# Hyperbolic attention: a constant product beside the points' products, inverses taken once per row and head, and half of batch 1's logarithms moved among batch 0's weights

## The reference

```python
q_hyp = _expmap0(qn)
k_hyp = _expmap0(kn)
inner = -jnp.einsum('bhti,bhsi->bhts', q_hyp[..., :1], k_hyp[..., :1]) + jnp.einsum('bhtd,bhsd->bhts', q_hyp[..., 1:], k_hyp[..., 1:])
mdot = jnp.maximum(-inner, 1.0 + 1e-06)
dist = jnp.arccosh(mdot)
scores_hyper = -(dist * dist) / curv_k
scores = (1.0 - alpha) * scores_euclid + alpha * scores_hyper
scores = jnp.where(causal[None, None], scores, -jnp.inf)
attn = jax.nn.softmax(scores, axis=-1) * spike_mask
y = jnp.einsum('bhts,bhsd->bhtd', attn, v)
```

## Time and profile before

| | us |
|---|---|
| runs of the kernel before | 2789.78, 2783.0, 2782.54 (median 2783.0) |
| the profiled execution: time, span | 2787.06, 2785.2 |
| TensorE busy in the span | 2356.0 (85%) |
| VectorE busy | 1455.3 (52%) |
| ScalarE busy | 1055.5 (38%) |
| POOL busy | 382.4 (14%) |
| the changed stage | 1560.4 to about 1664.3 of the span |

### The profile page before, as it was taken

The page is one execution under the profiler, slowest core; times in us unless marked ns, Lnnn a source line. Parts: engine busy times, 40 slices in busy tenths (PEclk is TensorE's granted clock), DMA queues, the critical chain, the costliest instruction groups (busy, mean ns, idle before and its releaser), DMA issues. The chain is left out here.

```text
span 2785.2 us, 38678 instructions
## 1 busy us (share of the span) xinstructions
PE 2356.0 (85%) x15024; PEld 1366.0 (49%) x15024; DVE 1455.3 (52%) x2285; ACT 1055.5 (38%) x1896; POOL 382.4 (14%) x659
## 2 busy tenths in 40 slices
PE   3999999868999598999996675976879799698778
PEld 1344444435699363444543442441227657364447
DVE  4777777323221366888881873335666433223333
ACT  2566666412111234777773561224222233021310
POOL 2453000000000300000001520003430000000100
PEclk8899999987999797999998677987688899898779
DMA  6976544020353898555430001001004430200200
GB/s 189 246 185 160 103 92 62 1 95 1 150 220 129 249 288 221 96 117 104 88 46 33 12 1 58 28 1 62 0 0 154 166 149 1 93 3 0 99 0 8
DMA packets 108213, 258.59 MB, mean 93 GB/s; under 512 B 11808, under 2 KB 83072, under 8 KB 94080
## 3 DMA queue, kind: packets, MB, share of 16 engines
q1 hardware_dynamic: 101696, 203.71, 27.7%
q0 software_dynamic: 2736, 39.37, 4.2%
q10 hardware_dynamic: 3600, 13.04, 1.2%
HBM read 211.26 MB, written 44.83 MB: 92 GB/s over the span
## 5 line engine op out<-in xcount | busy, mean ns | idle before, releaser
L666 DVE TENSOR_REDUCE sta_parts<-sta_psA 128x1 f32<-128x1024 f32 x544 | 625.7, 1187 | 186.9 <-PE sta_psA L583 185.2
L724 ACT ACTIVATE sta_probs<-sta_psS 128x512 f32<-128x512 f32 x1056 | 575.8, 596 | 274.2 <-PE sta_psS L594 272.1
L594 PE MATMUL sta_psS<-L_xattn_qS,L_xattn_kst 99*128 99x256 bf16 x2112 | 355.8, 278 | 11.5 <-ACT sta_probs L724 6.6
L583 PE MATMUL sta_psA<-L_xattn_kst,L_xattn_qS 99*128 99x512 bf16 x1088 | 293.2, 387 | 45.9 <-PEq L59 31.0
L594 PEld LDWEIGHTS sta_psS<-L_xattn_qS,L_xattn_kst 99*128 99x128 bf16 x2112 | 161.2, 98 | 259.3 <-ACT sta_probs L724 183.6
L603 PE MATMUL sta_psO<-sta_probs,L_xattna_V 128*32 128x256 f32 x2560 | 189.5, 385 | 0.0
L583 PEld LDWEIGHTS sta_psA<-L_xattn_kst,L_xattn_qS 99*128 99x128 bf16 x1088 | 104.2, 99 | 130.5 <-DVE sta_parts L666 43.8
L202 ACT ACT_TABLE_LOAD x14 | 18.0, 1283 | 331.6 <-PEq L59 331.6
L2385 PE MATMUL l2t_psY<-l2t_hc,top_consts_weights 128*128 128x512 f32 x128 | 96.4, 863 | 26.7 <-DVE l2t_hc L2436 26.6
L603 PE MATMUL sta_psO<-sta_probs,L_xattn_V 128*32 128x256 f32 x1536 | 114.5, 389 | 0.0
L1008 ACT ACTIVATE sht_probs<-sht_psS 128x768 f32<-128x768 f32 (+1 forms) x64 | 55.3, 864 | 148.6 <-PE sht_psS L852 99.8
(11 more groups left out here) (625 smaller groups left out, 3967.2 us busy)
## 6 DMA issues: line engine op xcount, KB each, us to landing
L_xattn_kst<-L_xattn_keys SPq DMA_DIRECT2D x186, 136.0 KB, 4.9
L_xattn_kst<-L_xattn_keys SPq DMA_DIRECT2D x186, 128.0 KB, 4.5
L_xattn_values<-prj_rows SPq DMA_DIRECT2D x64, 256.0 KB, 3.8
L_xattn_keys<-prj_parts SPq DMA_DIRECT2D x32, 384.0 KB, 4.0
L_xattna_V<-in_ctxV SPq DMA_DIRECT2D x5, 2048.0 KB, 11.8
L_xattna_V<-L_xattn_values SPq DMA_DIRECT2D x5, 2048.0 KB, 11.0
l2f_W<-in_M SPq DMA_DIRECT2D x10, 1024.0 KB, 7.6
L_xattn_keys<-sta_bparts SPq DMA_DIRECT2D x24, 384.0 KB, 7.3
```

Source lines behind the costliest of these rows:

```text
L583: last = nc.tensor.matmul(psA[:, u % 2, col:col + rhs.shape[1]], lhsT, rhs, start=True, stop=True)
L594: last = nc.tensor.matmul(psS[:, at % 2, j * T:(j + 1) * T], lhsT, rhs, start=True, stop=True)
L666: nc.vector.tensor_reduce(into(parts[:, u // n % 2]), view(psA[:, u % 2, :]), AX.X, ALU.max).then_inc(max_taken, 1)
L724: nc.scalar.activation(probs[:, u % NP, i * 512:(i + 1) * 512], psS[:, at % 2, :], ACT.Exp, scale=scale).then_inc(probs_ready, 1)
```

## The change

It does four things. First, the spikes are no longer spread at the start; the tile spikesT, the copy and the 512-column spreading are gone. Second, behind each pair's points' products TensorE multiplies the constant bf16 mask (128 x 512) by the identity, twice, into psY, where nobody reads it. Third, normalisation goes another way: TensorE makes the row sums of a quad as a 128 x 8 tile with queries on partitions (`sums`), VectorE takes the reciprocal of that and multiplies it by the spikes in two small operations (`invert`), ScalarE copies it to 128 x 256 with each number repeated 32 times (`widen`), TensorE turns that with two transposes (`spread`), and VectorE multiplies by yP (`scale`). psY now has one buffer, whose other half takes the sums, and psN has one. Fourth, ScalarE takes Ln of pairs 8 to 11 ahead of Exp of pair 4; only pairs 12 to 15 are left for after batch 0's weights.

```diff
@@ -1873,12 +1874,12 @@
         D = p.sb("D", [P, B * H, W])
         R = p.sb("R", [P, B * H, W])
         top = p.sb("top", [P, PAIRS, TB, 2])
-        spikesT = p.sb("spikesT", [P, NTOK])
         yP = p.sb("yP", [P, 2, T])
-        inverse = p.sb("inverse", [P, 2, T])
+        inverse = p.sb("inverse", [P, 2, TB, 4])
+        wide = p.sb("wide", [P, 2, T])
         banks = p.ps("banks", [P, 2 * SLOTS, 512])
-        psY = p.ps("psY", [P, 2, T])
-        psN = p.ps("psN", [P, 2, T])
+        psY = p.ps("psY", [P, 512])
+        psN = p.ps("psN", [P, T])
 
         def pair(kind, k):
             n = place[kind, k] % SLOTS
...
@@ -1935,29 +1936,35 @@
                     pe.wait_ge(turn_copied, 2 * g + 2)
                     if g:
                         pe.wait_ge(y_copied, g)
+                        pe.wait_ge(inverse_in, g)
                     b = g // (QUADS // B)
                     for kt in range(TB):
                         for j in range(4):
                             h = 4 * (g % (QUADS // B)) + j
-                            last = nc.tensor.matmul(psY[32 * j:32 * j + 32, g % 2, kt * P:T], v[:, b * TB + kt, 32 * h:32 * h + 32],
+                            last = nc.tensor.matmul(psY[32 * j:32 * j + 32, kt * P:T], v[:, b * TB + kt, 32 * h:32 * h + 32],
                                                     R[:, 4 * g + j, kt * T:kt * T + T - kt * P], start=kt == 0, stop=kt == TB - 1)
                     last.then_inc(y_ready, 1)
 
-                def spread_sums(g):
+                def sums(g):
+
                     pe.wait_ge(y_copied, g + 1)
+                    for t in range(TB):
+                        last = nc.tensor.matmul(psY[:, T + 4 * t:T + 4 * t + 4], yP[:, g % 2, t * P:(t + 1) * P], K["col32"], start=True, stop=True)
+                    last.then_inc(sums_ready, 1)
+
+                def spread(g):
+                    pe.wait_ge(widened, g + 1)
                     if g:
-                        pe.wait_ge(inverted, g)
-                    else:
-                        pe.wait_ge(spikes_copied, 1)
-                    nc.tensor.matmul(psN[:, g % 2, :], K["sel32"], yP[:, g % 2, :], start=True, stop=True).then_inc(spread_ready, 1)
-
-                for t in range(NT):
-                    last = nc.tensor.matmul(psN[:].rearrange("p a n -> p (a n)")[:, t * P:(t + 1) * P], spikes[:, t:t + 1].to_broadcast([P, P]), K["ident"],
-                                            start=True, stop=True)
-                last.then_inc(spikes_spread, 1)
+                        pe.wait_ge(scaled, g)
+                    for t in range(TB):
+                        last = nc.tensor.matmul(psN[:, t * P:(t + 1) * P], wide[:, g % 2, t * P:(t + 1) * P], K["ident"], start=True, stop=True)
+                    last.then_inc(spread_ready, 1)
+
                 for k in range(PAIRS):
                     slot_free("hyper", k)
                     products(pair("hyper", k), turned["qH"], turned["kH"], k, True).then_inc(hyper_ready, 1)
+                    for _ in range(2):
+                        nc.tensor.matmul(psY[:], K["ident16"], K["mask16_q"], start=True, stop=True)
                 for b in range(B):
                     first, end = b * HALF, (b + 1) * HALF
                     scores(first)
@@ -1968,10 +1975,14 @@
                         turn(k)
                         if k % 2 == 0 and k > first:
                             values(k // 2 - 1)
+                        if k % 2 == 0 and k > first + 2:
+                            spread(k // 2 - 2)
                         if k % 2 and k > first + 1:
-                            spread_sums((k - 3) // 2)
+                            sums((k - 3) // 2)
                     values(end // 2 - 1)
-                    spread_sums(end // 2 - 1)
+                    spread(end // 2 - 2)
+                    sums(end // 2 - 1)
+                    spread(end // 2 - 1)
 
             @block.vector
             def _(dve):
@@ -1985,14 +1996,19 @@
                     dve.wait_ge(reach_ready, k + 1)
                     V.scalar_tensor_tensor(out=both(R, k), in0=pair("hyper", k), scalar=1.0, in1=both(D, k), op0=ALU.add, op1=ALU.mult).then_inc(root_in, 1)
 
-                def normal(g):
+                def invert(g):
+                    b = g // (QUADS // B)
+                    dve.wait_ge(sums_ready, g + 1)
+                    V.reciprocal(inverse[:, g % 2], psY[:, T:T + 4 * TB].rearrange("p (t h) -> p t h", t=TB)).then_inc(inverse_in, 1)
+                    dve.wait_ge(inverse_in, g + 1)
+                    for t in range(TB):
+                        last = V.tensor_scalar(inverse[:, g % 2, t], inverse[:, g % 2, t], spikes[:, b * TB + t:b * TB + t + 1], None, ALU.mult)
+                    last.then_inc(inverted, 1)
+
+                def scale(g):
                     b, c = g // (QUADS // B), g % (QUADS // B)
                     dve.wait_ge(spread_ready, g + 1)
-                    V.reciprocal(inverse[:, g % 2, :], psN[:, g % 2, :]).then_inc(inverted, 1)
-                    dve.wait_ge(inverted, g + 1)
-                    V.tensor_tensor(inverse[:, g % 2, :], inverse[:, g % 2, :], spikesT[:, b * T:(b + 1) * T], ALU.mult).then_inc(inverse_ready, 1)
-                    dve.wait_ge(inverse_ready, g + 1)
-                    V.tensor_tensor(attT[:, c, b * T:(b + 1) * T], yP[:, g % 2, :], inverse[:, g % 2, :], ALU.mult).then_inc(scaled, 1)
+                    V.tensor_tensor(attT[:, c, b * T:(b + 1) * T], psN[:], yP[:, g % 2, :], ALU.mult).then_inc(scaled, 1)
 
                 reach(0)
                 for k in range(PAIRS):
@@ -2014,10 +2030,15 @@
                         for t in range(TB):
                             last = V.tensor_reduce(top[:, k, t, :], both(D, k)[:, :, cols[t]], AX.X, ALU.max, negate=True)
                         last.then_inc(top_ready, 1)
-                        if k % 2 and k >= first + 5:
-                            normal((k - 5) // 2)
-                    normal(end // 2 - 2)
-                    normal(end // 2 - 1)
+                        if k % 2 == 0 and k >= first + 4:
+                            invert(k // 2 - 2)
+                        if k % 2 == 0 and k >= first + 6:
+                            scale(k // 2 - 3)
+                    invert(end // 2 - 2)
+                    scale(end // 2 - 3)
+                    scale(end // 2 - 2)
+                    invert(end // 2 - 1)
+                    scale(end // 2 - 1)
                 dve.wait_ge(scaled, QUADS)
 
             @block.gpsimd
@@ -2037,8 +2058,8 @@
                         act.wait_ge(root_in, k + 1)
                         nc.scalar.activation(line(R, k), line(R, k), ACT.Sqrt).then_inc(root_ready, 1)
 
-                def logarithms(b):
-                    for k in range(b * HALF, (b + 1) * HALF):
+                def logarithms(pairs):
+                    for k in pairs:
                         act.wait_ge(sum_ready, k + 1)
                         nc.scalar.activation(line(D, k), line(D, k), ACT.Ln, bias=K["ones"][:, 0:1]).then_inc(log_ready, 1)
 
@@ -2050,11 +2071,18 @@
                     act.wait_ge(y_ready, g + 1)
                     if g >= 2:
                         act.wait_ge(scaled, g - 1)
-                    nc.scalar.copy(yP[:, g % 2, :], psY[:, g % 2, :]).then_inc(y_copied, 1)
+                    nc.scalar.copy(yP[:, g % 2, :], psY[:, 0:T]).then_inc(y_copied, 1)
+
+                def widen(g):
+                    act.wait_ge(inverted, g + 1)
+                    nc.scalar.copy(wide[:, g % 2, :].rearrange("p (x n) -> p x n", n=32),
+                                   inverse[:, g % 2].rearrange("p t h -> p (t h)").unsqueeze(2).to_broadcast([P, 4 * TB, 32])).then_inc(widened, 1)
 
                 def weights(b):
                     first, end = b * HALF, (b + 1) * HALF
                     for k in range(first, end):
+                        if b + 1 < B and k == first + HALF // 2:
+                            logarithms(range(end, end + HALF // 2))
                         act.wait_ge(top_ready, k + 1)
                         for j in range(2):
                             for t in range(TB):
@@ -2065,16 +2093,18 @@
                             copy_turned(k - 1)
                             if k % 2 and k > first + 1:
                                 copy_y((k - 3) // 2)
+                            if k % 2 and k >= first + 5:
+                                widen((k - 5) // 2)
                     copy_turned(end - 1)
+                    widen(end // 2 - 2)
                     copy_y(end // 2 - 1)
-
-                act.wait_ge(spikes_spread, 1)
-                nc.scalar.copy(spikesT[:], psN[:].rearrange("p a n -> p (a n)")).then_inc(spikes_copied, 1)
+                    widen(end // 2 - 1)
+
                 roots(0)
-                logarithms(0)
+                logarithms(range(HALF))
                 roots(1)
                 weights(0)
-                logarithms(1)
```

(13 more changed lines are left out.)

## The result

| | before | after |
|---|---|---|
| median of the runs, us | 2782.77 (2781.08 to 2789.78) | 2808.96 (2806.4 to 2827.57) |
| ratio after/before, 95% interval | | 1.0110 (1.0077 to 1.0142) |
| profiled execution, span, us | 2785.2 | 2804.2 |
| stage, from the first product to attT's last write, us | 103.8 | 126.7 |

A forecast was written before the change was run, and what follows sets the result against it. VectorE was taken to bound the points' products, and chains between engines the weights. Batch 0's +8.4 us (holding the opening's -0.9) and batch 1's +6.3 make +14.7: median 2783.0 to 2797.7 us (2792.9 to 2800.4); range with rivals 2787 to 2809.

The forecast's parts named there:

- part 3: Normalisation in both batches: VectorE saves 1.65 us per quad, but inverses wait for sums and spreadings for widening.
- Part 1: Opening and constant products: TensorE at 2.4 GHz, added matmuls hidden in its waits, Exp of pair 0 0.9 us earlier.
- the cold opening: Rival: TensorE at 1.2 GHz from the first pairs bounds the opening; total +26 us, 2809; chance 0.12.
- Part 2: Ln of pairs 8 to 11 ahead of Exp 4: +5.3 us there, 3.4 us back in the later block.
- A drain beside each load: Skill page's rule, weighed: about 1.38 us on top of each ScalarE table load; sum +17.4 us instead of +14.7.
- the chain of batch 0: Batch 0's weights from Exp 4 through quad 3's widening: 22.5 us, mostly at 1.2 GHz, against 16.0 before.
- the all-1.2 GHz value of 23.5: Batch 0's weights from Exp 4 to widen 3 if TensorE ran at 1.2 GHz throughout: 23.5 us; 19.8 at 2.4.
- the string: Step-by-step times of waits between engines, counted from Exp 4 in batch 0 and from Exp 8 in batch 1.
- The bound all at 1.2 GHz: Batch 1 from Exp 8 to the end, with 1.2 GHz from spread 4 on: 39.7 us; 38.0 was taken.
- Waits hidden: Rival: ScalarE packs Ln into idle time and TensorE's new waits lie beside other work; +1.9 us, 2785; chance 0.15.
- faster: Rival: waits hidden and VectorE's 1.65 us less per quad counts where it is gapless; -4.1 us, 2779; chance 0.08.
- the rival with more waits: Rival: more waits between engines than the prediction strung together; +18 to +22 us; chance 0.05.

The follow-up runs named there:

- reordered: The changed kernel with all its operations, normalisation steps put one or more pairs later, four buffers instead of two for yP, inverse and wide; stage 104.89 us, ratio 0.9993.
- transposed: The changed kernel with the two products of each spreading made as transposes instead of fp32 matmuls; stage 120.05 us, ratio 1.0061.
- clock_held: The changed kernel with further constant products wherever TensorE waits, ahead of the spreadings and of turns 0, 4 and 8; stage 110.40 us, ratio 1.0019.
- fill_before: The kernel before with constant products behind each pair's products and 20 and 26 more ahead of the batches' first turns; stage 94.04 us, ratio 0.9985.
- change_again: The changed kernel, unaltered, measured a second time against the kernel before; stage 126.70 us, median 2811.44 us, ratio 1.0076.
- norm_alone: The kernel before with only the new normalisation in the change's order and no spikes' spreading; no constant products, no moved Ln; stage 119.95 us, ratio 1.0049.
- fill_reordered: The reordered kernel with 20 and 26 constant products ahead of the first turns of batches 0 and 1; run twice, stages 99.04 and 99.02 us, ratio 0.9979 both times.
- fill_reordered_noln: The reordered kernel with constant products ahead of the first turns and Ln of pairs 8 to 11 not moved; stage 91.64 us, ratio 0.9952.

## Why the prediction was wrong in size, point by point

**Direction and mechanism: right.** Slower, by the two waits strung together in part 3, with VectorE's reciprocals waiting for TensorE and the spreadings for ScalarE. Undoing the order (reordered) takes 21.8 of the 22.8 us back, the clock's part included.

**Part 1: right.** Exp 0 was to come 0.9 us earlier, and came 0.87 (33.83 against 34.70). The clock held at 1.00 in the first part; the cold opening did not come. Which of the reasons that I gave for it held the clock, no run separates. That TensorE would be idle over 4 us ahead of turn 0 and start the weights at 1.2 GHz was right too: 4.35 us, and 0.55 in the row of 1592 to 1596.

**Part 2: right.** Exp 4 at 1612.25 (forecast 1612.5). The later block, from the last widening to Exp 8, took 6.02 (5.95). A drain beside each load was set aside on 1.31 us before, and the kernel after has the same:

```profile
1638.05 3.41 ACT L2064 ACTIVATE hyp_D<-hyp_D,top_consts_weights 128x768 f32<-128x768 f32 x4
...
1641.48 1.28 ACT L2090 ACT_TABLE_LOAD   x1
...
1642.77 1.49 ACT L2090 ACTIVATE hyp_D<-hyp_D,hyp_top 128x128 f32<-128x128 f32 x4
```

From the last Ln's end, 1641.46, to Exp 8 lie 1.31 us. By "ScalarE: Activation LUTs" in the Trainium skill, section "What ACT_TABLE_LOAD costs", it would be 2.66; no run here shows a drain.

**Part 3: the step that failed is the size of the chain.** Exp 8 was forecast at 1641.0 and came at 1642.77; the end at 1679.0, and it came at 1686.62. As the stage began 0.46 us earlier than before's, lengths compare better: the two terms are the chain of batch 0, 24.48 us instead of 22.5, and batch 1, 43.86 instead of 38.0. The 7.8 us are accounted for:
- Batch 0, 2.0 us, from Exp 4 to the end of quad 3's widening. One us is the choice of 22.5 over the all-1.2 GHz value of 23.5, the other a step left out of the string: spread 2 stands on TensorE between values 3 and sums 3. (Spreadings too cheap at 1.2 GHz and a spread 1 that ran at 2.4 cancel.)
- Batch 1, 5.9 us. From Exp 8 to pair 13's scores I had 14.95, with before's clock; it took 17.43 (1642.77 to 1660.20), at 0.50 throughout: 2.5. Of these 0.45 are there from the start, as TensorE was still at the scores of pair 10 when Exp 8 began, which I hadn't seen (values 4 at 10.92 after Exp 8, before 10.47); 2.05 are the clock, which before rose 11.5 us after Exp 8. From there on I took 38.0 between 35.9 and 39.7, and the clock was at 1.2 GHz almost to the end: 1.7. Spread 4 cost 1.01 instead of 0.55: 0.45. The tail has a spread 6 that the string left out, 1.02 us, and small change: 1.2.

The tail, in order of time:

```profile
1671.20 0.21 DVE L2002 RECIPROCAL hyp_inverse<-hyp_psY 128x8 f32<-128x8 f32 x1 [6.23 <-PE hyp_psY L1952]
...
1681.94 1.22 PE L1960 MATMUL hyp_psN<-top_consts_weights,hyp_wide 128*128 128x128 f32 x4
...
1682.96 0.85 PE L1952 MATMUL hyp_psY<-top_consts_weights,hyp_yP 128*128 128x4 f32 x4
```

So 4.75 of the 7.8 us are the clock, 2.0 two spreadings of the diff that I didn't walk past, 0.45 TensorE's late start into batch 1, 0.45 a matmul priced as a transpose, and the rest small change. This split is worked out along the two strings; the runs show the price of a spreading (transposed) and the clock's part of the whole stage (clock_held and fill_before), not each item. The bound all at 1.2 GHz that I wrote down took it only from spread 4 on; a batch whose TensorE is busy without pause at 0.50 had been in my own rows (the 32-row products of the earlier trace rows), and I used it for the opening and not for batch 1. What I wrote of the clock there, that it stays at 2.4 GHz where 128-row work stands among the 32-row products, the kernel after contradicts: it has both kinds in the 27.2 us at 0.50.

**The sum.** 10.45 for sums 1 is 10.35 by its own terms, which changes nothing. The rest of the program, which I took as unmoved, gave 3.8 us back in this profile and none in that of change_again; the last section shows at what clocks it runs. **The rivals.** Waits hidden and faster fall with the waits' rows, the cold opening with the clock of the first part. The first measurement's median, 2808.96, is the cold opening's 2809, by luck: its mechanism didn't happen. The stage's 22.8 lie just above the rival with more waits (+18 to +22), but for another reason: what was missing from the string was mostly instructions and the clock.

## What to carry to other kernels

Write the order of each engine down and walk every instruction of the diff along it: here a small reciprocal with its multiplies took its own half us where its input was old, and held VectorE idle for up to 7.10 us where its input was made by the instructions in front. When waits are added to TensorE's path, size the stage at the lower clock to its end as a case of its own, since the lower clock lengthens what stands between the waits. When filling TensorE's waits, fill them in the kernel before as well, or the clock's gain is put down to the change. A stage made shorter or longer by 10 us is judged by its own length as well as by the total, as the rest of the program varies by more.

## What the runs showed of the hardware

**Later stages with the same instructions run at another granted clock.** fill_before has a stage 9.8 us shorter, 0.35%, and a ratio of only 0.9985. Its profile, of the slowest of its 12 executions, spends 13.2 us more after the stage, with the same instructions. Stretches to the end of l2x and of l2s, before first, fill_before second:

```profile
1664.20:1859.10 194.90, 143.78 (x768) 76.27 (x768) 55.95 (x129) 32.16 (x48) 7.55 (x33) 0.82 0.08 31
1859.10:1894.20 35.10, 26.29 (x56) 10.63 (x56) 19.41 (x30) 8.05 (x13) 0.00 (x0) 0.84 0.00 1
```

```profile
1653.90:1852.40 198.50, 148.23 (x768) 79.81 (x768) 55.94 (x130) 32.17 (x48) 7.51 (x33) 0.79 0.08 31
1852.40:1890.90 38.50, 30.94 (x56) 11.73 (x56) 19.40 (x30) 8.05 (x13) 0.00 (x0) 0.72 0.00 0
```

The work is the same by the counts and by VectorE's and ScalarE's times; TensorE is granted 0.72 instead of 0.84 and its 56 products take 4.65 us longer. It isn't the shorter stage that brings this. norm_alone, whose stage is 16.1 us longer, has it too, and the kernel after, 22.8 longer, hasn't (the same stretch, norm_alone first):

```profile
1878.20:1916.70 38.50, 30.84 (x56) 11.69 (x56) 19.39 (x30) 8.05 (x13) 0.00 (x0) 0.72 0.00 0
```

```profile
1879.20:1914.30 35.10, 26.21 (x56) 10.65 (x56) 19.45 (x31) 8.05 (x13) 0.00 (x0) 0.84 0.00 0
```

The clock is also what the runs of one kernel differ by: of the 35 runs of before in the third group the fastest (2780.27) has a mean granted clock of 0.890, the slowest (2803.97) 0.879, and time and clock correlate at -0.95. What in an execution sets it was not found.

**A small VectorE operation lasted as long as POOL's.** The two 128x4 multiplies by the spikes take 0.36 us where POOL stands still. Beside its squares they took more, in clock_held most:

```profile
1602.80 7.27 DVE L2017 TENSOR_SCALAR hyp_inverse<-hyp_inverse,l1a_spikes 128x4 f32<-128x4 f32 x2
...
1604.13 5.77 POOL L2064 TENSOR_TENSOR hyp_R<-hyp_D 128x768 f32<-128x768 f32 x4
...
1609.97 1.38 DVE L2038 SCALAR_TENSOR_TENSOR hyp_D<-hyp_R,l1a_coef,hyp_banks 128x128 f32<-128x128 f32 x4
```

The first of the two took 7.13 us and ended at 1609.93, 0.03 after POOL's last square; pair 6's scores, queued behind them, make Exp 6 2.75 us late: without that, Exp 4 to Exp 8 would be 26.0, close to the 25.75 that the prediction gave for full clock. In the kernel after the pair took 2.81, under ScalarE's block, and cost nothing, as forecast from 1.85 us; in fill_reordered and its repeat the first took 5.90 and 5.92, again up to POOL's last square. In fill_reordered_noln both multiplies fell beside POOL's sum of root and m-1 and took 0.23 and 0.22, so not every POOL operation does it. That POOL holds them is read from the ends, which lie within 0.04 us of the end of a square; no run moved the squares away. The wider operations around them (scores' sum 1.38 for four, maxima 1.01 for two) keep their times beside POOL.
